# Gated cross-attention with a top-2 expert layer on one core: x loaded as 96 and 4 rows and asked for ahead of the keys, h stored in three late pieces, the spare rows zeroed behind the first of them

## What is computed

```python
def _L0_xattn_ref(query, key):
    a = jnp.einsum('bqd,bkd->bqk', query, key)
    e = jax.nn.softmax(a, axis=-1)
    c = jnp.einsum('bqk,bkd->bqd', e, key)
    return c

def _L0_ffn_ref(x, W_gate, b_gate, W_e, b_e):
    logits = x @ W_gate + b_gate
    _, top_idx = jax.lax.top_k(logits, TOP_K)
    y_all = jax.nn.relu(jnp.einsum('bsd,edh->bseh', x, W_e) + b_e)
    y = jnp.take_along_axis(y_all, top_idx[..., None], axis=2)
    return y.mean(axis=2)
x = x + jnp.tanh(g_xattn[0]) * _L0_xattn_ref(_layernorm(x, axis=-1), ctx_4096)
x = x + jnp.tanh(g_ffn[0]) * _L0_ffn_ref(_layernorm(x, axis=-1), L0_ffn_W_gate, L0_ffn_b_gate, L0_ffn_W_e, L0_ffn_b_e)
```

## Time and profile before

| | us |
|---|---|
| median of 3 runs | 353.36 |
| the three runs | 348.69, 353.36, 355.1 |
| the profiled execution, its own run time | 354.86 |
| its span | 353.1 |
| TensorE busy | 319.7 (91%) |
| VectorE busy | 207.3 (59%) |
| ScalarE busy | 123.2 (35%) |
| chain that ended last: TensorE 64%, DMA 21% | |

### The profile page before, as it was taken

How to read it: one execution, slowest core, us unless ns; L and a number is a source line. 1 busy time by engine, 2 the same in 40 slices (tenths; PEclk the granted TensorE clock), 3 DMA queues, 4 the chain that set the end, 5 groups by cost and what they waited for, 6 DMA issues and landing times.

```text
span 353.1 us, 4292 instructions
## 1 busy us (share of the span) xinstructions
PE 319.7 (91%) x1488; PEld 233.2 (66%) x1488; DVE 207.3 (59%) x448; ACT 123.2 (35%) x165; POOL 80.1 (23%) x94
## 2 busy tenths in 40 slices
PE   0986999989999699998999999999999999999940
PEld 0543466555654448877888788888888888888830
DVE  2217258666778768796484975755276666751220
ACT  2223434335445335511353645415031551331000
POOL 6002012110203201083233222520121233201110
PEclk9999999989999879999999999999999999999995
DMA  7999999989979794226999999899359889543313
GB/s 253 302 267 312 344 307 384 383 314 347 382 294 361 256 393 103 117 59 163 376 341 367 354 355 357 253 356 302 62 160 347 270 230 402 146 59 61 52 17 52
DMA packets 24190, 90.58 MB, mean 257 GB/s; under 512 B 2882, under 2 KB 2882, under 8 KB 24158
## 3 DMA queue, kind: packets, MB, share of 16 engines
q1 hardware_dynamic: 13662, 52.86, 42.3%
q0 software_dynamic: 7360, 25.47, 26.5%
q10 hardware_dynamic: 3136, 11.83, 9.9%
HBM read 73.63 MB, written 16.52 MB: 255 GB/s over the span
## 4 chain that ended last, share of the span: by engine, by line
PE 64%; DMA 21%; DVE 7%; ACT 2%; POOL 2%; issue 1%; SPq 1%; DVEq 0%; POOLq 0%
PE ps L434 42%; DMA raw<-in_L_ffn_W_e 15%; PE ps L348 7%; PE ps L368 6%; DMA kT<-in_ctx_cols 5%; PE ps L417 3%; DVE wl L857 2%; PE ps L388 2%; PE ps L379 1%; PE ps L339 1%; ACT wh L601 1%; DVE stats L709 1%; DVE y L869 1%; DVE xl L861 1%; SPq L287 0%
## 5 line engine op out<-in xcount | busy, mean ns | idle before, releaser
L857 DVE TENSOR_TENSOR wl<-raw,wh 128x1024 fp32r<-128x1024 f32 x64 | 75.8, 1219 | 17.8 <-ACT wh L601 17.6
L434 PE MATMUL ps<-wh,xh 128*128 128x512 f32 x256 | 81.8, 400 | 1.0 <-DVE xl L861 1.0
L434 PE MATMUL ps<-wh,xl 128*128 128x512 f32 x256 | 79.7, 392 | 0.0
L434 PE MATMUL ps<-wl,xh 128*128 128x512 f32 x256 | 79.1, 393 | 0.0
L601 ACT ACTIVATE wh<-raw 128x1024 fp32r<-128x1024 f32 x64 | 64.1, 1052 | 34.1 <-DMA raw<-in_L_ffn_W_e 25.7
L1032 POOL DMA_INDIRECT out_rows<-y,dst_token x16 | 31.2, 1951 | 112.5 <-DVE y L871 93.6
L434 PEld LDWEIGHTS ps<-wl,xh 128*128 128x128 f32 x256 | 47.9, 188 | 11.2 <-DVE wl L857 0.4
L434 PEld LDWEIGHTS ps<-wh,xl 128*128 128x128 f32 x256 | 48.1, 188 | 10.9
L434 PEld LDWEIGHTS ps<-wh,xh 128*128 128x128 f32 x256 | 46.4, 188 | 10.7 <-DVE xl L861 1.9
L348 PE MATMUL ps<-kT,qT 128*100 128x361 f32 x128 | 44.8, 505 | 4.4 <-DMA kT<-in_ctx_cols 3.5
L604 ACT ACTIVATE xh<-ps 128x1024 fp32r<-128x1024 f32 x16 | 16.4, 1022 | 85.9 <-PE ps L417 85.8
(11 more groups left out here) (120 smaller groups left out, 245.8 us busy)
## 6 DMA issues: line engine op xcount, KB each, us to landing
raw<-in_L_ffn_W_e SPq DMA_DIRECT2D x64, 512.0 KB, 10.1
kT<-in_ctx_cols SPq DMA_DIRECT2D x16, 722.0 KB, 19.2
ctx<-in_ctx ACTq DMA_DIRECT2D x8, 1024.0 KB, 13.5
bias<-in_L_ffn_b_e SPq DMA_DIRECT2D x8, 512.0 KB, 12.2
ctx<-in_ctx ACTq DMA_DIRECT2D x8, 420.0 KB, 16.9
out_rows<-x_all POOLq DMA_DIRECT2D x8, 400.0 KB, 9.2
hn_rows<-hn POOLq DMA_DIRECT2D x8, 400.0 KB, 8.7
x_all<-in_x SPq DMA_DIRECT2D x7, 400.0 KB
```

The source lines that it names most:

```text
L434: mm = nc.tensor.matmul(into[:, n * HB:(n + 1) * HB], rows[:, k, :], weights[:, k, n * HB:(n + 1) * HB], start=(k == 0 and c == first), st ...
L857: nc.vector.tensor_tensor(wl[e % 2][:, k, :], raw[e % 2][:, k, :], wh[e % 2][:, k, :], ALU.subtract).then_inc(s_wl, 1)
```

## The change

Four things. Each load of x becomes two DMAs, of rows 0 to 95 and of rows 96 to 99, on the same semaphore, and VectorE waits for 32 instead of 16. x of batch b+2 is asked for after the wait for the scores and ahead of the keys of batch b+1, where x of batch b+3 stood behind them. h is stored in three DMAs (batches 0 to 3, 4 to 6, and 7) instead of eight; the first is issued in step 7 of GpSimd's loop behind the store of hn of batch 6, the second at the start of step 8, the third behind the last store of hn. The two DMAs of zeros stand behind the first of them. The waits for stored h count 3 x 16 instead of 8 x 16.

```diff
+        STORES = ((0, HALF_B), (HALF_B, B - 1), (B - 1, B))
...
+            Q_SPREAD = Q // 16 * 16
+            X_PARTS = [(0, Q_SPREAD), (Q_SPREAD, Q)]
+
             def load_x(b):
-                sp.dma_start(x_all[:, b, :], x[b, :, :]).then_inc(s_x[b - 1], 16)
+                for first, end in X_PARTS:
+                    sp.dma_start(x_all[first:end, b, :], x[b, first:end, :]).then_inc(s_x[b - 1], 16)
...
             for h in range(2):
-                sp.dma_start(x_all[:, 0, h * 512:(h + 1) * 512], x[0, :, h * 512:(h + 1) * 512]).then_inc(s_x0[h], 16)
+                for first, end in X_PARTS:
+                    sp.dma_start(x_all[first:end, 0, h * 512:(h + 1) * 512], x[0, first:end, h * 512:(h + 1) * 512]
+                                 ).then_inc(s_x0[h], 16)
             load_keys(0)
             load_x(1)
             load_keys(1)
             load_x(2)
-            load_x(3)
-            sp.wait_ge(s_scores, 1)
-            load_keys(2)
-            load_x(4)
-            for b in range(2, B):
+            for b in range(1, B):
                 if b + 1 < B:
                     sp.wait_ge(s_scores, b)
+                    if b + 2 < B:
+                        load_x(b + 2)
                     load_keys(b + 1)
-                if b + 3 < B:
-                    load_x(b + 3)
                 for k in FIRST_CHUNKS.get(b + 1, ()):
                     load_weights(0, k)
...
             sp.wait_ge(s_hn, B)
-            sp.wait_ge(s_hstore, 16 * B)
+            sp.wait_ge(s_hstore, 16 * len(STORES))
...
-            def store_hidden(b):
-                pool.wait_ge(s_h, b + 1)
-                g.dma_start(out[b * Q:(b + 1) * Q, :], x_all[:, b, :]).then_inc(s_hstore, 16)
+            def store_hidden(first, end):
+                pool.wait_ge(s_h, end)
+                rows = out[first * Q:end * Q, :].rearrange("(b q) d -> q b d", q=Q)
+                g.dma_start(rows, x_all[:, first:end, :]).then_inc(s_hstore, 16)
...
-                store_hidden(s - 1)
+                if s == B:
+                    store_hidden(*STORES[1])
                 guess_root(s + 2, 0, 2 if s + 2 < B else 1)
                 store_normed(s - 1)
-                if s == 2:
+                if s == B:
+                    store_hidden(*STORES[2])
+                if s + 1 == B:
+                    store_hidden(*STORES[0])
                     for t in range(HALVES):
```

More of the change, by code:

```diff
@@ L712, in measure_query @@
                 if b > 0:
-                    dve.wait_ge(s_x[b - 1], 16)
+                    dve.wait_ge(s_x[b - 1], 32)
                 for h in range(2):
                     if b == 0:
-                        dve.wait_ge(s_x0[h], 16)
+                        dve.wait_ge(s_x0[h], 32)
                     last = measure(b, 1, h)
@@ L936, in _ @@
             split_tile(2)
-            dve.wait_ge(s_hstore, 16 * B)
+            dve.wait_ge(s_hstore, 16 * len(STORES))
             dve.wait_ge(s_hn, B)
@@ L1105, in _ @@
             pool.wait_ge(s_zero, 32)
-            pool.wait_ge(s_hstore, 16 * B)
+            pool.wait_ge(s_hstore, 16 * len(STORES))
             pool.wait_ge(s_hnstore, 16 * B)
```

## The result

Twenty runs of each, in turn on one chip: 356.52 us after (354.66 to 358.9), 355.33 before (348.69 to 360.31). The ratio is 1.0122, its interval 1.0092 to 1.0152: a small slowdown, inside the 2% that such a measurement tells from no change, where the forecast was a small gain. The three runs of before that the prediction had were on the low side of its spread. The profiled execution of after took 355.54 us (span 353.8), the one of before 354.86 (353.1).

The account below looks back on a forecast made before the run. TensorE was taken as the bound from about 131 us, so only stalls before that could go: 354.86 - 3.3 - 3.0 + 0.3 = 348.9 us on the profiled execution's scale, median put at 348.5, range 344.9 to 353.4.

Parts of the forecast that it names:

- Stall B: Attention stage, 66.67 to 83.30 us: ScalarE waits for weight chunk 1; moving stores late gains 3.3 us of 3.39.
- Stall A: Attention stage, 25.40 to 40.38 us: batch 2's scores wait for kT; splitting x gains 3.0 us of 3.55.
- a first stretch that moves well over 282 GB/s: Sign that the forecast is right: DMA traffic to 37.67 us moves well over 282 GB/s, or the stretch ends sooner.
- Asking x ahead: x loads before the keys of batches 2 to 6: cost 0, up to 1.9 us per batch if cover fails.
- Start: Kernel start: more x loads on SyncE may complete x of batch 0 later; charged 0.3 us, bounds 0 and 0.8.
- Sum of the stage: Attention stage: gains of 3.3 and 3.0 us less 0.3 us at the start, 6.0 us in all.
- Rival 4: More than the stalls: the clock dip of 118 to 136 us also goes; 345.5 us, chance 0.13.
- The late stores: Stores behind the last batches land at about 148 us, wanted at 151.4 before tile 2's gather: cost 0, bounds 0 and 9.
- Rival 2: Late stores replace the stalls at GpSimd's wait before gathers of tiles 2 and 3: slower, 357.3 us, chance 0.11.
- Rivals 1 and 3: Attention stage: only B goes, 351.9 us, chance 0.15; or nothing but a shift, 353.4 us, chance 0.08.
- the signs named against the forecast: ScalarE still waiting for weights, batch 2's scores over 1 us, tile 2's gather for h; TensorE idle growing after 131 us.

Follow-up runs that it names:

- the waits behind: Kernel after, with GpSimd's waits for stored h and zeros moved behind the gathers of tiles 2 and 3: 348.87, 349.8, 356.42 and 356.89 us.
- the zeros early: Kernel after, with the zeros stored behind batch 1 as before: 349.39 us, ratio 0.9861 to before.
- the gather put into the row: Kernel before, with the gather of tile 2 waiting until the first of VectorE's six wl is done: 361.93 us, ratio 1.0253.

## Why the prediction was wrong

- **Stall B, 3.3 us: right** in size (3.35), and the late stores do remove it alone (last keys 79.17). They are not the only thing that does: with x asked for ahead of the keys ScalarE's wait for the chunk went too, with every store where it was.
- **Stall A, 3.0 us: right for the split, wrong for the change.** With the split alone the step is 3.38 shorter. The whole change took 1.67 and left a wait of 1.47 in its profile. These are single profiles, and they scatter: the traces with 100 rows wait 2.4 to 3.6 us for these keys, and of the five with the loads of after two have no such wait (the waits behind, the zeros early) and three wait 1.3 to 2.9. The prediction's sign of a first stretch that moves well over 282 GB/s did not come (279 in after, 290 with the split alone); its other form, that the stretch ends sooner, did (35.66 against 37.67). So the needed bytes came sooner without a higher rate, as they would if less overtook them.
- **Asking x ahead, "Cost 0": wrong.** The bound of up to 1.9 us per batch if the cover fails was named; the cover (13 us) does not always hold at batches 2 and 5. It costs about 0.7% of the time. Of the Trainium skill's two rules that the prediction weighed (DMA: Bandwidth & Descriptors), the runs agree with the one on rows and engines ("Why a DMA increments its semaphore by 16 and not by 1": 100 rows on 10 engines, 96 on 16); the rule against small pieces did not show in this kernel, whose split with four small rows won 1.4%. No run split x into two pieces of another size, so that it is the multiple of 16 that wins, and not the second DMA, is argued and not shown.
- **Start, 0.3 us: not seen** (25.06 against 25.40), and too small to be seen: at this point the other traces stand between 24.6 and 27.2.
- **Sum of the stage, 6.0 us: right**, 6.56, partly by luck: A came short by 1.3, and the last batch brought 1.2, which the prediction had not counted; 118 to 136 us ran at clock 0.94 instead of 0.81. Rival 4's dip went in part.
- **The late stores, "Cost 0; bounds 0 and 9": this is the step that failed, and it cost 7.4.** The landing, "about 148", came out at 147.27, by luck: it was worked out as 9.9 MB at 360 GB/s, and 8.2 MB were moved from 118 to 150 us, the end of them at 129 GB/s with the DMA engines half busy. The two things wrong with the step are what it was held against. First, "it is wanted at 151.4" was read from the old trace, while everything behind the stage moves forward by the gain: by the forecast's own 6.0 to 145.4, as measured by 6.6 to 144.8. The sum had taken the gain and kept the old date. Second, the price of being late, which the next point has.
- **Rival 2 named the place, the releaser and the sign, and missed the price.** "The first 1 us late is free and then each costs one" gives 2 us for 3.2 late; it cost 7.4. 0.6 us behind the gather VectorE begins its row of six wl, and an indirect gather issued inside it comes out at the row's end. The row stood in the old trace, and so did its effect: gather 3, issued at 152.72 beside the row, took 6.97 us. It did not matter there, and so I did not read it. GpSimd's line of before and VectorE's:

```profile
152.72 6.97 POOL L1022 DMA_INDIRECT xg<-hn_rows,src_token  x1 [0.30 <-issue]
```

```profile
151.99 6.88 DVE L857 TENSOR_TENSOR wl<-raw,wh 128x1024 fp32r<-128x1024 f32 x6
```

Rivals 1 and 3 are out: more than B went, and it was no mere shift. Of the signs named against the forecast three came: the scores of batch 2 still waited over 1 us (1.47), the gather of tile 2 waited for h stored, and TensorE's idle time after 131 us grew.

Open: why the gather of tile 3 was let in behind the first of six when VectorE had waited for a semaphore ahead of its row; what the two runs at 356 us with the waits behind look like in a trace. That the last gain of 1.2 us in batch 7 comes from the clock is a reading of one profile, not tested.

## What to carry to other kernels

When a sum says that a stage ends sooner, every deadline behind that stage moves with it: hold late work against the new dates, and the slack that it lived in shrinks by exactly the gain. Then look at what begins next on the engines around the deadline; a wait that slips past the start of a long row of another engine can cost the row, not the slip, and a run-to-run time with two values is a sign of such an edge. A bundle of three edits whose sum is near nothing can hold one worth 1.4% (here x in 96 and 4 rows), one that costs 0.7% and one that is worth keeping in a smaller dose.

## What was not expected of the hardware

**An indirect gather is held by VectorE's row.** In every one of these kernels but one a gather whose issue began inside the row of six TENSOR_TENSOR (both inputs in SBUF) took 5.1 to 7.0 us instead of 1.04. It ended 0.8 to 0.95 us after the row: 153.18 against 152.24 in after, 158.82 against 157.90 with the gather put into the row. A single wl does the same on its own scale, as the kernel before shows later on, on GpSimd's timeline and on VectorE's:

```profile
193.13 1.81 POOL L1022 DMA_INDIRECT xg<-hn_rows,src_token  x1 [0.30 <-issue]
```

```profile
192.87 1.23 DVE L857 TENSOR_TENSOR wl<-raw,wh 128x1024 fp32r<-128x1024 f32 x1 [2.85 <-ACT wh L601]
```

**A store behind others lands late.** The last 400 KB of h took 3.2 us to land in before; in after 15.5, behind 4.3 MB on GpSimd's queue (1.64, 1.05, 1.23 and 0.41 of hn). The DMA issues of after in 115 to 133 us, the last column us from issue to landing:

```profile
out_rows<-x_all POOLq DMA_DIRECT2D x1, 1600.0 KB, 16.7
...
out_rows<-x_all POOLq DMA_DIRECT2D x1, 1200.0 KB, 20.0
out_rows<-zero POOLq DMA_DIRECT2D x2, 512.0 KB, 19.0
...
out_rows<-x_all POOLq DMA_DIRECT2D x1, 400.0 KB, 15.5
```

In 136 to 150 us the DMA engines were only half busy (0.50, 129 GB/s), so the end of that queue was not a matter of their total rate; what sets it is not shown. With the zeros out of it the same store took 9.3 us.

**An order of requests can matter without any change in bytes.** x of batch b+2 asked for ahead of the keys of batch b+1, same bytes and same pieces, cost 0.8% [0.25, 1.29] with 100 rows. It moved the lateness: ScalarE's wait of 3.87 us for a weight chunk went, and TensorE's waits of 1.45 and 1.64 us for the keys of batch 5 came.
